# Attention inside a macaron block: score and maxima tiles of two head pairs in one group of TensorE work, denominators behind the output projection

## The reference

```python
qkv = layernorm(x) @ w_qkv.T                        # 16 heads of 64
q = q * cos + rotate_half(q) * sin + fenc           # the same for k
attn = softmax(q @ k.T * 64 ** -0.5)                # 512 x 512 for each head
x = x + (attn @ v) @ w_out.T + b_out
```

## Time and profile before

| | |
|---|---|
| median of 3 runs | 1315.45 us (1312.94 to 1315.97) |
| the profiled execution | 1315.65 us |
| its span, first to last instruction | 1313.9 us |
| TensorE matmul busy | 1268.6 us, 97% |
| VectorE busy | 840.1 us, 64% |
| ScalarE busy | 614.2 us, 47% |
| GpSimd busy | 883.0 us, 67% |
| mean granted clock of TensorE | 0.987 of full |

### The profile page before, as it was taken

How to read it: one execution, slowest core, us unless ns; L and a number is a source line. 1 busy time by engine, 2 the same in 40 slices (tenths; PEclk the granted TensorE clock), 3 DMA queues, 4 the chain that set the end, 5 groups by cost and what they waited for, 6 DMA issues and landing times.

```text
span 1313.9 us, 21618 instructions
## 1 busy us (share of the span) xinstructions
PE 1268.6 (97%) x7858; PEld 790.6 (60%) x7858; DVE 840.1 (64%) x1352; ACT 614.2 (47%) x917; POOL 883.0 (67%) x652
## 2 busy tenths in 40 slices
PE   5999998699999999999999999999999999999998
PEld 3666665456565656666565656565565655666665
DVE  6656646876666666666666666677786664565632
ACT  3443532255545455545545554545545444443422
POOL 0443444678797888798888888788888862443343
PEclk9999999699999999999999999999999999999999
DMA  5344040223233232323232323323232321442240
GB/s 164 129 177 125 6 130 16 48 42 70 55 66 58 54 70 50 74 50 74 49 74 50 70 54 65 59 54 70 50 74 50 73 34 18 146 137 81 66 153 17
DMA packets 118681, 95.40 MB, mean 73 GB/s; under 512 B 75760, under 2 KB 85008, under 8 KB 118320
## 3 DMA queue, kind: packets, MB, share of 16 engines
q1 hardware_dynamic: 118576, 94.01, 29.8%
HBM read 57.53 MB, written 2.88 MB: 46 GB/s over the span
## 4 chain that ended last, share of the span: by engine, by line
PE 91%; DVE 5%; issue 2%; ACT 1%; DMA 1%; POOL 0%; SPq 0%; DVEq 0%; ACTq 0%
PE banks L1028 17%; PE banks L450 16%; PE banks L1011 13%; PE banks L463 10%; PE banks L1043 7%; PE banks L987 7%; PE banks L952 6%; PE banks L1016 4%; PE banks L1052 4%; PE banks L971 3%; PE banks L994 1%; DVE neg_max L1201 1%; PE banks L412 1%; PE banks L405 1%; PE banks L476 1%
## 5 line engine op out<-in xcount | busy, mean ns | idle before, releaser
L1201 DVE TENSOR_REDUCE neg_max<-banks 128x2 f32<-128x1024 f32 x256 | 313.2, 1224 | 103.1 <-PE banks L987 96.8
L1125 ACT ACTIVATE work<-banks 128x1024 f32<-128x1024 f32 x256 | 250.2, 1025 | 166.6 <-PE banks L1016 166.6
L1303 POOL TENSOR_TENSOR turn<-turn,side_turned 128x512 f32<-128x512 f32 x128 | 160.6, 1275 | 132.4 <-DMA side_turned<-side 132.3
L1028 PE MATMUL banks<-work 128*64 128x512 f32 x1024 | 233.9, 599 | 0.0
L1297 POOL TENSOR_TENSOR turn<-turn,fenc 128x512 f32<-128x512 f32 x128 | 161.9, 1287 | 14.9 <-DVE side L1194 10.9
L1308 POOL TENSOR_TENSOR qk_l<-turn,qk_h 128x512 fp32r<-128x512 f32 x128 | 162.0, 1287 | 0.9 <-ACT qk_h L1130 0.9
L1313 POOL TENSOR_TENSOR work<-work 128x1024 f32<-128x1024 f32 x64 | 152.8, 2387 | 11.2 <-PE banks L1028 11.2
L1028 PEld LDWEIGHTS banks<-work 128*64 128x64 f32 x1024 | 67.8, 136 | 132.9 <-issue 110.1
L987 PE MATMUL banks<-qk_h 64*128 64x512 f32 x512 | 118.0, 455 | 13.2 <-DVE neg_max L1201 10.2
L796 POOL TENSOR_TENSOR turn<-turn,work 128x512 f32<-128x512 f32 x56 | 72.2, 1294 | 87.1 <-DVE turn L717 87.1
L796 POOL TENSOR_TENSOR o_raw<-o_raw,work 128x512 f32<-128x512 f32 x52 | 66.8, 1288 | 89.2 <-DVE o_raw L717 89.2
(11 more groups left out here) (169 smaller groups left out, 2364.6 us busy)
## 6 DMA issues: line engine op xcount, KB each, us to landing
work<-share SPq DMA_DIRECT2D x32, 1024.0 KB, 9.3
side_turned<-side SPq DMA_DIRECT2D x256, 128.0 KB, 3.1
rec_all<-rec_d SPq DMA_DIRECT2D x128, 128.0 KB, 3.3
x_tok<-in_x SPq DMA_DIRECT2D x8, 256.0 KB, 6.1
out<-x_tok SPq DMA_DIRECT2D x8, 256.0 KB, 9.2
work<-in_w_gate_up SPq DMA_DIRECT2D x1, 1280.0 KB, 7.8
work<-in_w_qk SPq DMA_DIRECT2D x1, 1024.0 KB, 9.5
den_d<-den_rows SPq DMA_DIRECT2D x64, 4.0 KB
```

The costliest lines, as they stand in the source:

```text
L1028: ins = nc.tensor.matmul(O[OWN[h], :], v_all[:, kt, n * DH:(n + 1) * DH], pt[:, g % 2, kt, h * T:(h + 1) * T], start=(kt == 0), stop=(kt = ...
L1125: nc.scalar.activation(pt[:, g % 2, kt, :], S[kt].rearrange("p h q -> p (h q)"), ACT.Exp, scale=QSCALE).then_inc(s["probs"], 1)
L1201: nc.vector.tensor_reduce(neg_max[:, g % 2, qt::DH], M2, AX.X, ALU.max, negate=True).then_inc(s["maxes"], 1)
L1303: nc.gpsimd.tensor_tensor(turn[:, g % 2, part], turn[:, g % 2, part], side_turned[:, part], ALU.add).then_inc(done, 1)
```

## The change

Each tile of scores changes place by half a turn: `S` gives banks 2 and 3 to key quarters 0 and 2, and 0 and 1 to quarters 1 and 3. The third maxima tile of a pair goes to banks 6 and 7 (`OW`), which the output product and the denominators use otherwise. On TensorE the last two score tiles of a pair move from the end of period p to the start of period p+1, and all four maxima tiles of pair p+1 stand in period p, around them and the first two score tiles. The denominators follow the output projection. ScalarE's exponentials and its copy of the denominators move with these; VectorE takes all four maxima first in a period; GpSimd normalizes first and adds its partial sum ahead of the low halves; SyncE's copy of the denominators moves to the start of the next period. Some of the waits change their counts.

```diff
--- before.py
+++ after.py
@@ -851,8 +851,9 @@
                 "y_ps", "y_done", "bias_added", "early_roped", "norms", "first_applied", "first_sum", "early_norm")}
             rec_in = (sem("att_rec_in0"), sem("att_rec_in1"))
             SA, SB, M2 = (banks[:, i:i + 2, :] for i in (0, 2, 4))
-            S = (SA, SB, SB, SA)
-            O, W = bank[6], bank[7]
+            S = (SB, SA, SB, SA)
+            O, W, OW = bank[6], bank[7], banks[:, 6:8, :]
+            M = (M2, M2, OW, M2)
             KQ, MT, XT = SA, SB[:, 0, 0:P], SB[:, 1, :]
             OWN = (slice(0, DH), slice(DH, P))
             Q, K = 0, 1
@@ -974,7 +975,7 @@
                 def project_both(g, p):
                     pe.wait_ge(s["x_lo_ready"], g // PAIRS + 1)
                     pe.wait_ge(s["roped"], g)
-                    at_least(pe, s["probs"], p * TT + 1)
+                    at_least(pe, s["probs"], p * TT + 2)
                     project(g, K, KQ[:, K, :])
                     project(g, Q, KQ[:, Q, :]).then_inc(s["qk_ps"], 1)
 
@@ -982,28 +983,38 @@
                     if qt == 0:
                         pe.wait_ge(s["k_high"], g + 1)
                         pe.wait_ge(s["q_high"], g + 1)
-                    at_least(pe, s["maxes"], g * TT + qt)
+                    if qt == 2:
+                        pe.wait_ge(s["v_ready"], min(g + 2, B * 2 * TT))
+                        at_least(pe, s["den_copied"], g - 2)
+                        at_least(pe, s["y_done"], g - 4)
+                    else:
+                        at_least(pe, s["maxes"], g * TT + (qt if qt < 2 else 2))
                     for h in range(2):
-                        ins = nc.tensor.matmul(M2[:, h, :], qk_h[OWN[h], g % SETS, Q, qt * P:(qt + 1) * P],
+                        ins = nc.tensor.matmul(M[qt][:, h, :], qk_h[OWN[h], g % SETS, Q, qt * P:(qt + 1) * P],
                                                qk_h[OWN[h], g % SETS, K, :], start=True, stop=True)
...
                     pe.wait_ge(s["maxes"], (g + 1) * TT)
-                    at_least(pe, s["probs"], p * TT + 2)
+                    at_least(pe, s["probs"], p * TT + 1)
                     nc.tensor.transpose(MT, neg_max[:, g % 2, :], ident[:]).then_inc(s["shift_ps"], 1)
...
                         pe.wait_ge(s["low"], g + 1)
-                    if kt == 0:
-                        at_least(pe, s["probs"], n)
+                        at_least(pe, s["probs"], n - 1)
+                    if kt == 0 and g == 0:
+                        pe.wait_ge(s["shift_ready"], 1)
+                    if kt == 1:
+                        at_least(pe, s["probs"], n - 1)
+                        pe.wait_ge(s["roped"], min(g + 3, N))
                     if kt == 2:
-                        pe.wait_ge(s["probs"], n)
+                        pe.wait_ge(s["probs"], n - 1)
                         pe.wait_ge(s["shift_ready"], min(g + 2, N))
                         pe.wait_ge(s["x_lo_ready"], min((g + 4) // PAIRS + 1, B))
                     if kt == 3:
+                        pe.wait_ge(s["probs"], n - 1)
                         pe.wait_ge(s["roped"], min(g + 4, N))
                     keys = slice(kt * P, (kt + 1) * P)
                     for i, (k, q) in enumerate(((qk_h, qk_h), (qk_h, qk_l), (qk_l, qk_h))):
@@ -1021,6 +1032,7 @@
                     if kt == 0:
                         pe.wait_ge(s["probs"], (g + 1) * TT)
                         pe.wait_ge(s["v_ready"], min(g + TT, B * 2 * TT))
+                        pe.wait_ge(s["maxes"], min((g + 3) * TT - 1, N * TT))
                         at_least(pe, s["o_copied"], g)
                         at_least(pe, s["y_done"], g - 2)
                     for h in range(2):
@@ -1054,8 +1066,14 @@
                     ins.then_inc(s["y_ps"], 1)
 
                 def period(p):
-                    new, ahead, nxt, last = p + 3, p + 2, p + 1, p - 1
+                    new, nxt, last = p + 3, p + 1, p - 1
                     if exists(nxt):
+                        maxima(nxt, 0)
+                    if exists(last):
+                        scores(last, 2)
+                        scores(last, 3)
+                    if exists(nxt):
+                        maxima(nxt, 1)
                         maxima(nxt, 2)
                     if exists(p):
                         scores(p, 0)
@@ -1083,13 +1101,6 @@
                         values(p)
                     if exists(p - 3):
                         project_out(p - 3, p)
-                    if exists(ahead):
-                        maxima(ahead, 0)
-                    if exists(p):
-                        scores(p, 2)
-                        scores(p, 3)
-                    if exists(ahead):
-                        maxima(ahead, 1)
                     if exists(last):
                         denominators(last, p)
 
@@ -1097,6 +1108,8 @@
                     pe.wait_ge(ffn1["x_done"], B)
                     for p in PERIODS:
                         period(p)
+                    scores(N - 1, 2)
+                    scores(N - 1, 3)
                     for kt in range(TT):
                         apply_v(N - 1, kt)
                 elif tail == 0:
@@ -1150,6 +1163,11 @@
 
                 def period(p):
                     ahead, last = p + 2, p - 1
+                    if exists(p - 2):
+                        copy_den(p - 2)
+                    if exists(last):
+                        exponentials(last, 2)
+                        exponentials(last, 3)
                     if exists(p):
                         exponentials(p, 0)
                         exponentials(p, 1)
@@ -1168,19 +1186,16 @@
                         x_high(front_at(p))
                     if value_tile(p):
                         values(p)
-                    if exists(p):
-                        exponentials(p, 2)
-                        exponentials(p, 3)
                     if front_at(p + 1) is not None:
                         normalise_tokens(front_at(p + 1))
-                    if exists(last):
-                        copy_den(last)
-                    if p == JOIN_LOGITS_AT:
-                        ffn2["scalar"](act, "exps")
 
...
                         period(p)
+                    copy_den(N - 2)
+                    exponentials(N - 1, 2)
+                    exponentials(N - 1, 3)
+                    ffn2["scalar"](act, "exps")
                     copy_o(N - 1)
                 elif tail == 0:
                     copy_den(N - 1)
@@ -1198,7 +1213,7 @@
                     dve.wait_ge(s["max_ps"], g * TT + qt + 1)
                     if qt == 0:
                         at_least(dve, s["shift_ps"], g - 1)
-                    nc.vector.tensor_reduce(neg_max[:, g % 2, qt::DH], M2, AX.X, ALU.max,
+                    nc.vector.tensor_reduce(neg_max[:, g % 2, qt::DH], M[qt], AX.X, ALU.max,
                                             negate=True).then_inc(s["maxes"], 1)
 
                 def spread_maxima(g):
@@ -1243,18 +1258,16 @@
                         small_steps(p, i)
 
                 def period(p):
-                    new, ahead, nxt, last = p + 3, p + 2, p + 1, p - 1
+                    new, nxt = p + 3, p + 1
                     if exists(nxt):
-                        maxima(nxt, 2)
-                    norm(p, 0)
-                    if exists(nxt):
-                        maxima(nxt, 3)
+                        for qt in range(TT):
+                            maxima(nxt, qt)
                     if p in STATS_AT:
                         statistics(p)
-                    norm(p, 1)
                     if exists(p - 2):
                         reciprocals(p - 2)
-                    norm(p, 2)
+                    for i in range(3):
+                        norm(p, i)
                     if p in JOIN_NORM_AT:
                         ffn2["vector"](dve, p)
                     if exists(nxt):
@@ -1330,16 +1340,16 @@
                     new, ahead = p + 3, p + 2
                     if exists(p) and p % PAIRS == 1:
                         bias(p // PAIRS)
+                    if exists(p - 3):
+                        normalise(p - 3)
                     if exists(ahead):
                         turned_part(ahead, K, s["k_sum"], 1)
                         turned_part(ahead, Q, s["q_sum"], 2)
-                    if exists(p - 3):
-                        normalise(p - 3)
+                    if exists(p - 1):
+                        first_sum(p - 1)
                     if exists(ahead):
                         low(ahead, K, s["k_high"])
                         low(ahead, Q, s["q_high"]).then_inc(s["low"], 1)
-                    if exists(p - 1):
-                        first_sum(p - 1)
                     if exists(new):
                         fourier_part(new, K, s["roped"], 1)
                         fourier_part(new, Q, s["roped"], 2)
@@ -1390,12 +1400,12 @@
                     return
                 for p in PERIODS:
```

(5 more changed lines are left out.)

## The result

The changed kernel takes **1324.39 us** (median of 5 runs, 1322.26 to 1327.04), the kernel before 1315.45 (5 runs beside them, 1312.94 to 1315.97): ratio 1.0074, with a 95% interval of 1.0055 to 1.0093. It is slower by 8.9 us. The forecast was 1312.2, its range ended at 1321: both direction and range were missed.

A forecast was written before the change was run, and what follows sets the result against it. TensorE, busy throughout the attention loop, was taken as the bound. Steady periods +1.2 us (-0.20 passages, +0.22 wait, 58 periods) and the other places made -3.3 from 1315.65, and the median 0.20 lower: 1312.2; range 1306 to 1321.

The forecast's parts named there:

- TensorE starts 0.05 after the reduction that it waited for: Output product in the steady period: starts at 5.05, behind a reduction ending at 5.00, so it waits 0.22 us.
- The spare 0.1: Third score tile of a period: its banks are released at 2.55 us, and it comes at 2.65.
- Exponential 3 ends 0.93 later: ScalarE in the steady period: the next exponential's end, for a tile wanted at 3.58; clears by only 0.1 us.
- the passages: TensorE's changes of matmul form in a steady period: two fall away, one comes in, 0.33 - 0.12, rounded to 0.20 us saved.
- the new passage: Output projection to denominators on TensorE, absent from the trace before: costs 0.12 us, at most 0.21.
- The second rival: Steady period: passage saved is worth less and the product pays drain after its wait; period 13.47, 1320.8 us; chance 0.16.
- The first rival: Steady period: the output product's wait does not bite; period 13.10, whole 1299.4 us; chance 0.12.
- Start: First pairs: fewer rounds through banks 4 and 5 gain 2.0 us, the first two periods 0.4 more.
- Periods 47 to 50: Period 47, second feed-forward block's norm steps: now behind all four reductions, with the rotation 1.8 us to spare; saves 1.5 us.
- Period 61: Product 60 to 61, VectorE busy with tokens: 13.3 in place of 15.67, less up to 0.9 for the clock; saves 1.9 us.
- End: Last score tiles come directly ahead of the last product: 10.15 for 8.94, +1.2 us; period 62 adds 0.15.
- The third rival: Steady period as forecast, but no gains at start, 47 and 61: 1316.7 us, or 1314.5 with half; chance 0.22.

The follow-up runs named there:

- the experiment where nothing hid these slips: Changed kernel with the second maxima tile, not the third, in the output banks, between the last pair's score tiles: 1318.39 us, ratio 1.0014 to the kernel before.
- the half exponentials: Changed kernel with the second maxima tile in the output banks and half of each exponential left out in the steady periods: 1304.78 us, ratio 0.9908.
- maxima third: Changed kernel, output product's five waits reordered in the steady periods so that the compiled list has the maxima third: 1319.97 us, one run.
- maxima first of five: Changed kernel, output product's five waits reordered in the steady periods so that the compiled list has the maxima first: 1325.51 us, one run.
- the one with the spread: Kernel before, with the second feed-forward block's norm steps ahead of the reciprocals and spread over periods 46 to 58: 1314.71 us, ratio 0.9993.

## Why the prediction was wrong

**The step that failed** is in the steady period: "TensorE starts 0.05 after the reduction that it waited for". The number is right for its row: that is a maxima matmul with this one wait. It was carried over to the output product, which carries four waits besides, and there it is 0.21. The period is 0.155 over the forecast, and over the 58 periods that the prediction counts these are 9.0 of the 12.2 us between forecast and median. The waits of before and their number stood in the code; that a satisfied wait could cost was not asked. One wait alone gives 13.31 for the forecast's 13.32. This is shown, by seven kernels that differ in nothing but the waits of this product.

**A second use of the 0.05** failed too, and cost nothing. The exponential that frees the banks of the third score tile ends at 2.50, as its terms say, but the tile is released 0.148 behind it, at 2.65. The spare 0.1 was not there, and the step to the tile's second pair is 0.30 instead of 0.23 (709.18 to 709.48). As the prediction says, a slip of up to 0.22 is hidden there. Its "Exponential 3 ends 0.93 later" should be 1.03, the length of an exponential. In the experiment where nothing hid these slips they came to 0.24.

**Rightly forecast:** the passages (0.20; 0.19 by the half exponentials), the new passage (0.10 over its pitch), the reductions (2.63, 3.77 and 4.99), that the product waits for the second of them. **The second rival** named the period exactly, 13.47, and 1320.8 us, but for the wrong reason: its passage was not dearer, and no drain was paid behind the wait (0.054 with one wait). **The first rival** has its period of 13.10 only when exponentials are left out.

**The other terms.** Products are counted from 0; "before" and "after" are the profiled executions.

- *Start*, forecast -2.4 with the end of the first two periods (its terms for the first pair, 8.44 less 6.66, give -1.8 and not -1.9): product 4 starts at 317.52 before, 319.57 after, +2.0. But five experiments have the same first periods as the changed kernel (one wait, two, four, maxima third, maxima first of five), and there it starts at 315.8 to 319.2; with the changed kernel's the mean is 317.4. The two profiles with the old order (the kernel before and the one with the spread, 316.99) have 317.3. So no gain is shown, +0.2 for the forecast's -2.4. (The granted clock in the stretch from 230 to 262 us was 0.69 before, 0.75 after, 0.80 with one wait and 0.68 with four, so it scatters between executions too; it was not tested apart.) Product 0 does come earlier (260.74 for 263.70); the next three periods take 14.35, 15.36 and 15.25 for 13.36, 13.44 and 13.30. VectorE in the second of them:

```profile
277.67 0.20 DVE L1230 RECIPROCAL rec_c<-den_c 128x8 f32<-128x8 f32 x1 [1.64 <-DMA den_c<-den_d]
277.79 0.46 DVE L283 TENSOR_TENSOR nt<-ve,rs 128x28 f32<-128x28 f32 x1
278.17 2.41 DVE L284 TENSOR_SCALAR nt<-rs 128x28 f32<-128x28 f32 x1
280.62 1.21 DVE L286 TENSOR_TENSOR nt<-nt,rs 128x28 f32<-128x28 f32 x1
281.86 1.21 DVE L288 SCALAR_TENSOR_TENSOR rs<-nt 128x28 f32<-128x28 f32 x1
282.99 0.68 DVE L1222 TENSOR_TENSOR shift<-banks,own_rows 128x512 fp32r<-128x512 f32 x1
```

  GpSimd beside it:

```profile
278.16 2.39 POOL L1323 TENSOR_TENSOR work<-work 128x1024 f32<-128x1024 f32 x1
280.50 2.52 POOL L1318 TENSOR_TENSOR qk_l<-turn,qk_h 128x512 fp32r<-128x512 f32 x2
```

  The reciprocal waits for the transfer, four small steps follow, and shift and rotation after them; TensorE's scores wait for the rotation. The prediction let the second pair's gain go for this, and not the first's. That putting the steps ahead of the reciprocal mends it in the median was not shown. What makes these places scatter can be read from the traces: the step L284 starts just behind a GpSimd instruction and ends 0.03 behind it, 2.41 us later, and the next two steps end 0.04 behind the two GpSimd instructions that follow. This holds in all traces (last section), so a step costs anything from 0.17 to 2.4 us by how it falls beside GpSimd's queue.
- *Periods 47 to 50*, forecast -1.5: beyond four steady periods they take 1.45 us before, 2.61 after, and 0.03 to 1.57 in the same five experiments, mean of the six 1.3: -0.2. The steps stand behind the four reductions, but ahead of the rotation and so of the next period's reductions. TensorE waits for both:

```profile
897.54 0.50 PE L1022 MATMUL banks<-qk_h 64*128 64x512 f32 x2 [0.23 <-DVE side L1209]
...
899.31 0.73 PE L993 MATMUL banks<-qk_h 64*128 64x512 f32 x4 [0.57 <-DVE neg_max L1216]
```

  The run with two waits lost nothing there (0.03): its step L270 took 0.16 us, that of the changed kernel 2.35 beside a GpSimd instruction. In the three profiles with the spread nothing is lost, in either order.
- *Period 61*, forecast -1.9: 12.47 for 15.66, -3.2, and 12.46 to 12.58 in those five. The prediction feared a fall of the clock after the change (up to 0.9); it is in the kernel before that the clock falls there, to a mean of 0.70 of full (between its levels of 1.2 and 2.4 GHz) from 1075 to 1078 us, where TensorE waits 1.9 us for a reduction. Before and after, from product 60 to 61 (columns as in the earlier trace rows):

```profile
1066.31:1081.98 15.67, 13.27 (x92) 6.86 (x90) 10.19 (x11) 7.57 (x13) 9.20 (x7) 0.89 0.13 18
```

```profile
1079.30:1091.76 12.46, 11.57 (x89) 6.66 (x90) 9.15 (x12) 7.76 (x13) 7.95 (x6) 1.00 0.15 24
```

  So part of this gain is the clock's. A mean of 0.89 over 15.67 us can have cost at most some 1.7 us, an estimate from these two rows; the share was not tested.
- *End*, forecast +1.35: 10.13 for the last period (10.15 forecast), 12.54 for the one before (12.17): +1.56.

Together 9.7 (the 56 periods from product 4 to 60 at +0.174, by the mean from product 5 to 46, 13.526 for 13.352) + 0.2 - 0.2 - 3.2 + 1.6 = **+8.1**, against 8.9 between the medians. The rest, 0.8, is within what runs of one kernel differ by. The third rival, no side gains, was true of two of the three places. Its 1316.7 leaves out the end, +1.35, which does not depend on those gains; with it, it is 1318.0.

## What to carry to other kernels

Before a wait is added to an instruction that already has some, count them. In these traces the release grows from 0.055 to between 0.15 and 0.26 us when the wait that ends last isn't on the instruction itself. In a period that repeats 58 times this is more than the change was meant to bring. Write the wait that ends last so that it comes last in the compiled list (here, first in the code), or leave out those that earlier waits imply. And where a gain at one place shows in one profiled execution, look at the same place in the profiles of sibling kernels before you believe it: here the start of one product was spread over 4 us. Small VectorE steps are not short by nature; look what GpSimd does when they start.

## What the runs showed of the hardware

- A matmul whose late wait is on its weight load starts 0.053 to 0.055 us after the end of what it waits for, a reduction or an exponential. If the late wait is on a semaphore instruction ahead, it costs 0.09 more, and a second such instruction behind that one 0.11 more. If their waits are met early they cost nothing: in the run with the maxima written first they started 1.08 and 0.97 us ahead of the reduction's end.
- The order of the waits in the code sets that of the compiled list, but is not the same: five waits, numbered as written, came out as [4 3][5 2] 1, four as [3][4 2] 1. The first written is on the weight load.
- The profile puts the same gap down to "issue" (8.3 us, 40 times, in the changed kernel) or to the reduction, by where the wait stands. In the run with the maxima first of five the line is:

```profile
PE banks L1048 <- DVE neg_max L1224: 10.0, 39, 0.3
```

- Small VectorE steps of 128 x 28 values took anything from 0.16 to 2.41 us in the same kernel (L284). What they ran slow beside is GpSimd. The 14 traces hold 2166 norm steps (L268 to L288) that no GpSimd instruction overlaps; their median is 0.17 us and the longest took 0.20. Another 440 started under a GpSimd instruction with over 0.2 us left to run, and 438 of them ended 0.02 to 0.08 us behind its end, however long that took. The reciprocals (128 x 8, one input) ran under GpSimd instructions in 0.20. This is read from the records; no experiment moved GpSimd's work.
